# The experts' second matrices multiplied with the output projection once, their outputs weighed and summed in token layout, and the loop over images turned round

## What is computed

```python
weights  = softmax((nx @ Wq) @ (p @ Wk).T / 16)            # 1024 x 77
combined = concat(nx, weights @ (p @ Wv), anchor)          # 1024 x 768
probs    = softmax(combined @ router_W + router_b)         # 1024 x 3
h        = silu(combined @ e_w1[e] + e_b1[e])              # 1024 x 512 for each of 3 experts
routed   = sum over e of probs[:, e] * (h[e] @ e_w2[e] + e_b2[e])
g        = sigmoid(silu(combined @ gate_w1 + gate_b1) @ gate_w2 + gate_b2)
x        = x + g * (routed @ out_w + out_b)
```

## Time and profile before

| | |
|---|---|
| median of 3 runs | 4265.18 us (4250.13 to 4273.27) |
| the profiled execution's own time | 4247.97 us |
| its span, first to last instruction | 4246.2 us |
| mean granted TensorE clock | 0.959 |
| busy: PE, ACT, DVE, POOL | 90%, 55%, 50%, 17% of the span |

### The profile page before, as it was taken

One profiled execution on the slowest core, in us unless ns is written; L12 is line 12 of the kernel. 1 busy time (PEld: TensorE's weight loads), 2 busy tenths in 40 slices (PEclk: granted clock), 3 DMA queues, 4 the chain that ended last, 5 costly groups with the idle time before them and its releaser, 6 DMA issues.

```text
span 4246.2 us, 65032 instructions
## 1 busy us (share of the span) xinstructions
PE 3811.6 (90%) x19697; PEld 2171.6 (51%) x19697; DVE 2120.0 (50%) x3461; ACT 2326.9 (55%) x3970; POOL 712.1 (17%) x448
## 2 busy tenths in 40 slices
PE   6999999799898898998998979989988799999988
PEld 4555655334643474346534644356346543564366
DVE  2112120584368454753584447644855477438554
ACT  2122221476467645765576447755765477547754
POOL 2000000101410241004102310024005110140041
PEclk9999999899999999998999989999999899999999
DMA  3000000200000001000000010000000100010000
GB/s 112 19 23 20 11 20 11 69 2 26 31 11 2 12 31 40 2 26 31 11 2 11 31 41 1 17 31 21 1 11 31 41 1 17 11 40 2 1 31 21
DMA packets 90317, 92.57 MB, mean 22 GB/s; under 512 B 28246, under 2 KB 78364, under 8 KB 89884
## 3 DMA queue, kind: packets, MB, share of 16 engines
q1 hardware_dynamic: 61204, 63.43, 4.6%
q10 hardware_dynamic: 28808, 25.17, 1.9%
HBM read 77.80 MB, written 9.44 MB: 21 GB/s over the span
## 4 chain that ended last, share of the span: by engine, by line
issue 85%; POOL 13%; PE 1%; DMA 0%; POOLq 0%; SPq 0%; DVE 0%; ACT 0%; DVEq 0%; ACTq 0%
POOL hidl L1651 3%; POOL x L1642 2%; POOL ql L1669 2%; POOL small L1590 2%; POOL hTl L1597 1%; POOL kl L1669 1%; PE ps L618 1%; POOL W2h L1660 1%; POOL W1h L1660 1%; POOL W2l L1662 0%; POOL W1l L1662 0%; DMA gw<-in_L_gate_w 0%; POOL ew1h L1607 0%; PE ps L1044 0%; SPq L575 0%
## 5 line engine op out<-in xcount | busy, mean ns | idle before, releaser
L1306 ACT ACTIVATE probs<-ps 128x512 f32<-128x512 f32 (+1 forms) x2176 | 1214.1, 635 | 381.9 <-PE ps L618 377.9
L1552 DVE TENSOR_REDUCE mxh<-ps 128x2 f32<-128x1024 f32 x1024 | 1202.6, 1220 | 270.3 <-PE ps L618 270.3
L618 PE MATMUL ps<-probs,v 128*32 128x512 f32 (+1 forms) x4864 | 658.8, 614 | 1.4 <-ACT probs L1306 1.4
L618 PE MATMUL ps<-qs,ks 64*128 64x512 f32 x2048 | 529.8, 472 | 0.0
L1590 POOL TENSOR_TENSOR small<-small 128x4 f32<-128x4 f32 x64 | 66.9, 1046 | 2755.4 <-DVE small L1351 2755.4
L618 PE MATMUL ps<-ks,qs 64*128 64x512 f32 x2048 | 412.7, 454 | 113.3 <-DVE mxh L1552 87.0
L618 PEld LDWEIGHTS ps<-qs,ks 64*128 64x128 f32 x2048 | 254.9, 185 | 490.6 <-ACT probs L1306 349.4
L618 PEld LDWEIGHTS ps<-ks,qs 64*128 64x128 f32 x2048 | 194.5, 183 | 317.1 <-DVE mxh L1552 243.0
L1279 ACT ACTIVATE qs<-ps,cols 128x512 fp32r<-128x512 f32 x320 | 213.6, 689 | 79.8 <-PE ps L618 78.8
L618 PE MATMUL ps<-hT,slot 128*128 128x512 f32 x448 | 222.6, 639 | 37.3 <-ACT hT L1111 35.1
L1549 DVE TENSOR_REDUCE mx<-ps 128x4 f32<-128x312 f32 x384 | 164.3, 477 | 143.2 <-PE ps L618 140.9
(11 more groups left out here) (210 smaller groups left out, 5960.7 us busy)
## 6 DMA issues: line engine op xcount, KB each, us to landing
qs<-mrow SPq DMA_DIRECT2D x640, 2.0 KB, 1.7
slot<-in_L_w SPq DMA_DIRECT2D x8, 1024.0 KB, 6.5
slot<-in_L_fc_w SPq DMA_DIRECT2D x8, 1024.0 KB, 5.4
adw<-in_L_adaln_w SPq DMA_DIRECT2D x4, 1536.0 KB, 6.5
xin<-in_x ACTq DMA_DIRECT2D x5, 1024.0 KB, 5.4
x_after_block<-x ACTq DMA_DIRECT2D x20, 256.0 KB, 2.2
xin<-x_after_block ACTq DMA_DIRECT2D x5, 1024.0 KB, 5.4
ew<-in_L_e_w SPq DMA_DIRECT2D x6, 768.0 KB, 13.4
```

What stands on the lines that cost most here:

```text
L618: return pe.matmul(out, lhsT, rhs, start=start, stop=stop)
L1306: ins = act.activation(dst, src, ACT.Exp, scale=SCALE)
L1552: dve.tensor_reduce(mxh[:, z, t, j // 2, j % 2, :], ps[:, a:a + 2, :], AX.X, ALU.max, negate=True).then_inc(dve_done, M.add(dve_done, name))
```

## The change

- The products of the experts' second matrices with `outw` are made once, ahead of the loop (`W2o`, 24 products), and split in `W2oh` and `W2ol`. The biases are multiplied with `outw` once as well, and spread over the partitions (`b2o`, `rrow`, `grow`).
- rt and o are replaced by `expert_output(n, e)`: for each half, expert and 128 tokens, 12 fp32r products with the hidden units as the stationary operand and `W2oh` or `W2ol` (256 columns) as the moving one. The result has the tokens in the partitions. DVE multiplies it there with the token's probability and adds it to `acc` (`accumulate`); `base` starts `acc` with the biases.
- pb and pT go, with DVE's multiplications into `hid0`. The gate's bias is added by DVE.
- ACT applies silu to each expert block twice, to write `hidh0` and the whole `hid0`, and POOL makes `hidl0`.
- `EXPERT_ORDER` sets the order of the work for all engines: H are the hidden blocks, O an expert's output, G the gate, K the keys and `a` of the next image.
- The loop is turned round: kv, a, the normalisation and `turn` of an image are done at the end of the image before it; the first image's are done ahead of the loop, and those done in the last image are not used. At the loop's head PE waits for all that ACT and DVE did in the image before.
- Each image's residual x is loaded after the stores of the image before it, now at the loop's head on ACT's queue. SP's first loads for the loop `blocks` wait for POOL's last work of the experts' loop too.

```diff
+EXPERT_ORDER = [("H", 0, 0), ("H", 0, 1), ("O", 0, 0), ("H", 0, 2), ("O", 0, 1), ("H", 0, E), ("O", 0, 2), ("H", 1, 0), ("G", 0, 0),
+                ("H", 1, 1), ("O", 1, 0), ("H", 1, E), ("O", 1, 1), ("H", 1, 2), ("K", 1, 0), ("G", 1, 0), ("O", 1, 2)]
...
+            keys_of(before, "pre", "first")
+            queries_of(before, "pre")
+            pe.wait_ge(experts_loaded["fold"], 2 * LOADED)
+            for i in range(RM // 2):
+                b, act_was, dve_was = take(("W2o", i), dve=("W2ol", i))
+                pe.wait_ge(act_done, before(act_done, *act_was))
+                pe.wait_ge(dve_done, before(dve_done, *dve_was))
+                for j in range(2):
+                    m = 2 * i + j
+                    for k in range(KC):
+                        ins = mm(ps[:, b, j * D:(j + 1) * D], ew2T[:, k, m * P:(m + 1) * P], outw[:, k, :], k == 0, k == KC - 1)
+                ins.then_inc(mm_done, M.add(mm_done, ("W2o", i)))
...
+            turn(before, "pre")
...
+                def expert_output(n, e):
+                    z = (E * n + e) % 2
+                    for i2 in range(2):
+                        b, act_was, dve_was = take(("L0", "O", n, e, i2), dve=("L0", "acc", n, e, i2))
+                        pe.wait_ge(act_done, upto(act_done, *act_was))
+                        pe.wait_ge(dve_done, upto(dve_done, *dve_was))
+                        pe.wait_ge(pool_done, upto(pool_done, ("L0", "lo", n, 4 * e + 3)))
+                        for i in range(2):
+                            tt = slice((2 * i2 + i) * P, (2 * i2 + i + 1) * P)
+                            products = [(h[:, z, c, tt], w[:, 4 * e + c, :]) for c in range(4)
+                                        for h, w in ((hidh0, W2oh), (hidl0, W2oh), (hidh0, W2ol))]
+                            for c, (h, w) in enumerate(products):
+                                ins = mm(ps[:, b, i * D:(i + 1) * D], h, w, c == 0, c == len(products) - 1)
+                        ins.then_inc(mm_done, M.add(mm_done, ("L0", "O", n, e, i2)))
...
-                            mm(ps[:, b, i * D:(i + 1) * D], *pick("out_b"), True, False)
...
+                                ins = mm(ps[:, b, i * D:(i + 1) * D], hidg[:, k, tt], gw2[:, k, :], k == 0, k == KC - 1)
...
-                            for i in range(TPH):
-                                ins = mm(ps[:, b, i * P:(i + 1) * P], lg[:, TPH * n + i, e:e + 1].to_broadcast([P, P]), ident[:])
-                            ins.then_inc(mm_done, M.add(mm_done, ("L0", "pb", n, e)))
...
-                            mm(ps[:, b, i * D:(i + 1) * D], *pick("gate_b2"), True, False)
...
-                        mm(ps[:, b, :], eb2[:, c * P:(c + 1) * P], pT[:, half], True, False)
-                        for m in range(RM):
-                            if c == 0:
-                                pe.wait_ge(dve_done, upto(dve_done, ("L0", "hp", n, m)))
-                            ins = mm(ps[:, b, :], ew2[:, m, c * P:(c + 1) * P], hid0[:, m, :], False, m == RM - 1)
-                        ins.then_inc(mm_done, M.add(mm_done, ("L0", "rt", n, c)))
...
+                for kind, n, e in EXPERT_ORDER:
+                    if kind == "H":
+                        for m in range(4 * e, min(4 * e + 4, RM + GM)):
+                            evidence(n, m, early[m] if (n, e) == (0, 0) else hidden(n, m))
+                    elif kind == "O":
+                        expert_output(n, e)
+                    elif kind == "G":
+                        gate_output(n)
+                    else:
+                        keys_of(upto, "next", "experts")
+                        queries_of(upto, "next")
+                turn(upto, "ln0")
...
+                act.wait_ge(dve_done, upto(dve_done))
+                load_tokens(it + 1, "tokens")
+                act.wait_ge(x_stored, upto(x_stored))
...
+                            act.activation(hidh0[:, (E * n + e) % 2, m % 4, :], src, ACT.Silu, bias=col("L0_e_b1", m))
+                            act.wait_ge(pool_done, upto(pool_done, *turned[-4:-3]))
+                            act.activation(hid0[:, m % 4, :], src, ACT.Silu, bias=col("L0_e_b1", m)
+                                           ).then_inc(act_done, M.add(act_done, ("L0", "h", n, m)))
+                            turned.append(("L0", "lo", n, m))
...
+                    elif kind == "K":
+                        store(upto, it, 0)
+                        keys_of(upto, "next")
...
-                        dve.tensor_tensor(hid0[:, m, :], hid0[:, m, :], pb[:, m // 4, :], ALU.mult
-                                          ).then_inc(dve_done, M.add(dve_done, ("L0", "hp", n, m)))
...
+                def accumulate(n, e, i2):
+                    b = M.where(("L0", "O", n, e, i2))
+                    dve.wait_ge(mm_done, upto(mm_done, ("L0", "O", n, e, i2)))
+                    for i in range(2):
+                        t = TPH * n + 2 * i2 + i
+                        dve.wait_ge(dve_done, upto(dve_done, ("L0", "acc", n, e - 1, i2) if e else ("L0", "base", t, E - 1)))
+                        ins = dve.scalar_tensor_tensor(so_far(t), ps[:, b, i * D:(i + 1) * D], lg[:, t, e:e + 1], so_far(t), ALU.mult, ALU.add)
+                    ins.then_inc(dve_done, M.add(dve_done, ("L0", "acc", n, e, i2)))
...
+                            pool.tensor_tensor(hidl0[:, (E * n + e) % 2, m % 4, :], hid0[:, m % 4, :], hidh0[:, (E * n + e) % 2, m % 4, :].bitcast(F32),
+                                               ALU.subtract).then_inc(pool_done, M.add(pool_done, ("L0", "lo", n, m)))
```

More of the change, by code:

```diff
@@ L432, in build @@
         ctxT = place("ctxT", [P, KC, SP_])
-        ctxk = place("ctxk", [S, D])
         kvT = place("kvT", [P, KC, SP_])
@@ L1366, in _, with before @@
             dve.wait_ge(dve_done, 1)
+            def before(sem, *steps):
+                return M.upto("experts", 0, sem, steps) if steps else 1
+            for i in range(RM // 2):
+                dve.wait_ge(act_done, before(act_done, ("W2oh", i)))
+                part = slice(2 * i, 2 * i + 2)
+                dve.tensor_tensor(W2ol[:, part, :], ps[:, M.where(("W2o", i)), :].rearrange("p (i d) -> p i d", i=2), W2oh[:, part, :].bitcast(F32),
+                                  ALU.subtract).then_inc(dve_done, M.add(dve_done, ("W2ol", i)))
+            for i, parts in enumerate((b2o[0:2], [b2o[2], rrow], [grow])):
+                dve.wait_ge(mm_done, before(mm_done, ("biases", i)))
+                for j, part in enumerate(parts):
+                    ins = dve.tensor_copy(part[:], ps[:, M.where(("biases", i)), j * D:(j + 1) * D])
+                ins.then_inc(dve_done, M.add(dve_done, ("biases", i)))
+            dve.wait_ge(xin_loaded, LOADED)
+            for h in range(NH):
+                for t in range(TPH * h, TPH * h + TPH):
+                    stats(before, "pre", t, xin)
+                spread(before, "pre", h, 1e-5)
+            for h in range(NH):
+                normalise(before, "pre", h, xin)
             M.open("experts")
@@ new lines, in _ @@
+                start(0)
+                for kind, n, e in EXPERT_ORDER:
+                    if kind == "O":
+                        for i2 in range(2):
+                            accumulate(n, e, i2)
+                            if (n, e) == (1, E - 1):
+                                finish(1, i2)
+                    if (kind, n, e) == ("O", 1, 0):
+                        dve.wait_ge(xin_loaded, upto(xin_loaded, "tokens"))
+                        for h in range(NH):
+                            for t in range(TPH * h, TPH * h + TPH):
+                                stats(upto, "ln0", t, xin)
+                            spread(upto, "ln0", h, 1e-5)
+                    if kind == "G" and n:
+                        dve.wait_ge(pool_done, upto(pool_done, ("L0", "lo", 1, RM - 1)))
+                        for h in range(NH):
+                            normalise(upto, "ln0", h, xin)
+                    if kind == "G":
+                        gates(n)
+                    if (kind, n) == ("G", 0):
+                        finish(0, 0)
+                        finish(0, 1)
+                        start(1)
```

302 lines of the change are left out of this document (160 added, 142 removed).

## The result

The changed kernel takes 4084.68 us (median of four runs, 4082.39 to 4100.97) against 4258.74 us before (4250.13 to 4273.27): ratio 0.9596, 95% interval 0.9557 to 0.9635. The profiled execution took 4085.28 us, its span is 4083.5.

A forecast was written before the change was run, and what follows sets the result against it. PE's own pace bounds the experts' loop. Start 73, three images of 145.2, a last body of 116.1 and 4.2 of low clock give 628.9, 120.9 less, with the end 122.9: profiled 4125, median 4142 us (4100 to 4182).

The forecast's parts named there:

- The loop `blocks` has the same instructions: The loop behind the experts' loop: same instructions, so its length stays 4246.2 - 766.91 = 3479 us.
- The offset of 17 us: Whole kernel: the median lies 17 us above the profiled execution, before (4265.18, 4247.97) and after (4142, 4125).
- The experts' loop: From the start to PE's last output in the experts' part: ends at 628.9 in place of 749.75, 120.9 us less.
- Low clock: Experts' images: half clock behind the softmax's products (2.5 us) and the K wait (1.7), 4.2 an image.
- The turn: Between two images' experts' work: 24.9 us in place of 30.0, with s at 5.4 and u at 12.9.
- The end: Passage to `blocks`: DVE starts 15 us behind PE's last output in place of 17.2, taken as 2 us less.
- in their shadow: At the start: POOL's large subtractions (6.65 + 1.3) and the tokens' four end at 58, hidden; first hidden product at 73.
- The turning itself gives nothing net: Experts' loop: turning it round gives 5.1 us in the turn and takes 5.1 in the body.
- POOL's late rest: Rival, chance 0.07: POOL's `hidl` comes late, 2.7 us at each of 24 outputs, 65 in all: 4207.
- outputs at half clock: Rival, chance 0.05: all 288 output products of an image at 0.209 us, 26 us an image, 104 in all: 4246.
- The rival on the slower side: Chance 0.02: the experts' whole body at 1.2 GHz, over 100 us an image against 36 saved, 4400.
- Full clock nearly throughout and K's wait hidden: Rival, chance 0.12: image 141 - 2, last body 115, start 70; PE's experts' part ends at 602, 150 less, 4115.

The follow-up runs named there:

- b_act31: The kernel before with 31 more idle instructions at the start of ACT's program; ratio to before 0.9968.
- b_all: The kernel before with idle waits at the start of four programs: 31 on ACT, 77 on PE, 114 on DVE, 54 on POOL; ratio 0.9965.
- b_act6: The kernel before with only 6 more idle instructions in ACT's program; one execution, 4265.92 us beside 4252.42 before.
- a_act225: The changed kernel with 225 more idle instructions in ACT's program ahead of the loop `blocks`; ratio to before 0.9686.
- after_again: The changed kernel once more, unchanged, with a profile of its own; ratio to before 0.9605, profiled execution 4097.81 us.
- a_turn: As a_scores, with the next image's 16 transposes ahead of the last expert's output in place of behind it; 4072.76 us, ratio to before 0.957.
- a_scores: The changed kernel with the next image's s done right behind its transposes, waiting only for its own half's scaled tokens; ratio to before 0.9614.
- a_pool2: The changed kernel with POOL making each expert block's rest (`hidl0`) twice; ratio to before 0.9624.

## Why the prediction was right or wrong

The forecast was 57 us too high. Four things make it up.

- **"The loop `blocks` has the same instructions"** is the step that failed. It has, but not the same length. 13.5 us of the 25 are a stall of ACT behind the loop's jump back, which the shift of ACT's code removed; shown by taking it away (b_act31, b_all, b_act6) and bringing it back (a_act225). That the stall is the loading of instructions is argued, from the boundary and from the transfer in the gap. The other 11.6 are chance, as far as is known, not the change: after_again shows 12.6 us between two executions of the same program, by where the low clock fell. Between the profiles of before and of the changed kernel PE's busy time in `blocks` differs by 7.8 of these 11.6 (3119.4 and 3111.6).
- **The offset of 17 us** from the profiled execution to the median was carried over as if it were the kernel's. It wasn't: the profiled execution of before was a quick one among its runs (4247.97, the median 4265.18), that of the changed kernel (4085.28) lies at its median (4084.68). 17.6 us. Nor was 4265.18 firm: the same kernel's later medians are 4253.29 (23 runs), 4251.12 (7) and 4268.18 (11).
- **The experts' loop** was mis-sized by 12.0 of 120.9, with the mechanism right: the start was 1.9 us later than forecast, the four bodies took 19.3 less and their low clock 3.0 less, the three turns 8.4 more. Body without low clock: 186.19 - 74.91 = 111.3, forecast 116.1. Of this the keys and `a` took 607.73 - 604.35 = 3.4 for 5.1 (the wait was 0.52 for 1.2, and there was no half clock; the forecast's own parts, 1.9, 1.2 and 1.8, make only 4.9), the gate 611.04 - 607.73 = 3.3 for 4.2 in each half. That is 3.5 of the 4.8; the rest is spread. The output products were priced right: (102.13 - 96.61) / 46 = 0.1200 us in five of an image's six groups, (616.75 - 611.35) / 46 = 0.1174 in the last, forecast 0.1195. Low clock costs 115.9 - 111.3 = 4.6 us in the body of images 1 to 3 and nothing in the first; 4.2 was forecast for each, 1.7 of it behind the keys, where there is none. The turn took 27.7, forecast 24.9: the wait of 4.3 was forecast at 4.6, but s took 6.8 for 5.4, and u 14.8 for 12.9, both at half clock in part.
- **The end** gave 4.8 in place of 2, 2.8 us of the error (rounding apart). The forecast kept the landing of xin as the last link; now DVE comes straight from its memset, which ends at 629.35, and xin is there.

The start, 73 for 74.9, was right by accident: "in their shadow" was said of POOL's subtractions, and they held up DVE by 9 us.

"The turning itself gives nothing net" was right for how it was written: 3.4 + 27.7 = 31.1 now, 30.0 and up to 4 of low clock before. a_turn shows that this was a matter of where the transposes stand: put ahead of the last output, with s straight behind it, they take 10.9 us off an image (s and its waits alone, a_scores, 3.5).

Of the rivals, POOL's late rest (a_pool2) and outputs at half clock (0.12 and 0.1174) are refuted for this kernel; the second one's mechanism is real, for the one output that did wait, in a_pool2, was followed by 0.213 us a product, as in the earlier trace rows. The rival on the slower side named 4400, which its own terms don't give: 100 us in each of four images on top of 4142 is 4542. "Full clock nearly throughout and K's wait hidden" was half right, on the side of K. The range was too narrow because it had no term for `blocks` beyond the runs' own spread, although it named another length of `blocks` as the thing that would make it wrong.

## What to carry to other kernels

Code that isn't touched can still change its time when its place in an engine's program moves: compare the length of the untouched stages first, and take an "issue" gap behind a loop's jump back for a sign that the place of the code matters; a few idle instructions ahead of the loop show whether it is so. Fill a wait with work that is ready (the transposes ahead of the last output) rather than shorten it, for a short wait brought the half clock as well. And a forecast for a median must not carry over the luck of the one execution that was profiled.

## What the runs showed of the hardware

- ACT stands still for about 6 us at a jump back of the loop `blocks` even without the gap: from the end of its last issue to that of ctxT it is 1634.92 - 1628.32 = 6.6 us before and 1495.21 - 1489.27 = 5.9 after. No run removed this part. Before and in a_act225, where the loop's code lies 256 instructions apart, a second stall of 4.1 us (4.71 - 0.57) follows; 6 instructions more or 31 more, and it is gone.
- POOL and DVE hold each other up, in both directions. In a_turn the operation that adds to x takes 0.69 us alone and 1.65 beside POOL's subtractions, and these take 5.91 for four, where they take 2.49 for two otherwise:

```profile
583.24 1.65 DVE L1524 SCALAR_TENSOR_TENSOR x<-sg,x 128x512 f32<-128x512 f32 x1
...
586.61 0.69 DVE L1524 SCALAR_TENSOR_TENSOR x<-sg,x 128x512 f32<-128x512 f32 x1
```

- The prediction named `base` and POOL's `hidl` as such a pair and said that no row showed it. The changed kernel's trace does, in the view of the tile `b2o` (ns, least, median and most): the longest `base` operations take 1.52 us for 0.48, while four subtractions of POOL take 5.52 (at 226.32) where one takes 1.27. No output waited for either, so PE lost nothing by it.

```profile
L1485 DVE SCALAR_TENSOR_TENSOR acc<-b2o,lg,acc x64: 471/480/1523, 86.9 to 582.5; 128x256 f32<-128x256 f32 x64
```

- A wait of 0.5 us (for kv0T) was not followed by the half clock; those of 0.67 behind 1.64, of 2.2 and of 4.3 were. Why two executions of one program get different low stretches in `blocks`, and the kernel before, with and without idle instructions, in its experts' loop (images 177 to 188 us apart), stays open.
